# Feed-forward and routing of a graph layer: block 2's second layers ahead of block 3's first, routing steps moved up, ranks in another PSUM bank

## The chip, the core and the metric

One core of a Trainium2 chip runs the whole program. The metric is the device time of one execution in microseconds; the kernel before takes 1076.64 us (median of 3 runs, 1076.25 to 1078.03).

## What is computed

A graph layer over 2048 nodes of width 256 and a mixture of 8 experts behind it, both with a residual. The changed stage is the end of the first and the beginning of the second: the feed-forward of the graph layer, the layer norm behind it, and the routing of each node to its two best experts.

```python
    # graph layer: attention over adj, then
    ht = layer_norm(ht + attn, ln2_scale, ln2_bias)
    ff = gelu_tanh(ht @ W1) @ W2                 # W1 256x1024, W2 1024x256
    x = x + ht + ff
    # mixture of experts, on the normalised rows
    xn = _layernorm(x)
    gate_logits = xn @ gate_w.T                  # 8 experts
    topk_vals, topk_idx = top_k(gate_logits, 2)
    topk_w = softmax(topk_vals)
    for e in range(8):
        y = gelu(xn @ w1[e].T + b1[e]) @ w2[e].T + b2[e]
        out += comb[:, e:e + 1] * y              # comb: topk_w at topk_idx
    return x + out
```

## The kernel before

The program has two blocks of instruction streams, one stream for each engine, with semaphores between them written out by hand; at the end of a block every engine drains and all wait for each other. The first block does the attention (to about 660 us) and then the feed-forward and the routing; the second runs the experts over 23 slots of 256 or 128 rows.

The feed-forward works on four blocks b of 512 nodes (four tiles of 128, TPB). For block b:

- TensorE turns the normalised rows (turn_h2), makes the eight parts f of the hidden layer (hidden, six products each, in fp16 pairs) into PSUM banks 0 and 1, and the second layer for two halves r of the block (back, 48 products each, banks 4 and 5).
- ScalarE copies the turned rows (high_turned) and does the Gelu and the fp16 copy of each part f (hidden_high); VectorE makes the low half of each (split_turned, split_hidden). back(b, 0) needs all eight splits of its block. The split products of even and odd blocks lie in the places of expert weights 1 and 2 (gT[0], gT[1]), so SyncE loads expert set 1 behind back(2, 1) and set 2 behind back(3, 1).
- VectorE adds the second layer (ffn_sum), forms the new x (new_x), its moments (new_stats, new_moments); GpSimd makes the row factors from them (row_factors(1, b)); ScalarE normalises the four tiles (normalise_x) into rows, which has a buffer for even and one for odd blocks.
- TensorE turns the rows (turn_xn, banks 2 and 3), ScalarE copies them (copy_xnT), TensorE makes the gate logits (gates, bank 2).
- VectorE chooses the best and the second expert (choose_first, choose_second); TensorE counts the ranks of the nodes in each expert (ranks, bank 3); ScalarE makes the exponential of the gap between the two logits (gap_exponential); VectorE computes the weights and the target rows (send: slots).
- GpSimd scatters the rows to expert_rows, eight indirect DMAs for a block (scatter). normalise_x(b) for b of 2 or 3 waits until the scatter of block b - 2, which has the same buffer of rows, has landed.

The order in which each engine does these things is the order of the calls in its stream. Before, TensorE does turn_h2(3), the eight parts of hidden(3) with ranks(0) behind f = 4, back(2, 0), turn_xn(1), back(2, 1), gates(1), back(3, 0), ranks(1), back(3, 1), turn_xn(2), gates(2), ranks(2), turn_xn(3), gates(3), ranks(3). Since ranks(b) and the turned rows share bank 3, turn_xn(b) waits until VectorE has read the ranks of block b - 1 in send (rank_read; its last writer is place, L1159). ScalarE's exponentials need another activation table than the Gelus.

Of the kernel before, what the change touches and what calls it, by code (L numbers as in the profile page):

```python
# [6 lines left out]
ALU = mybir.AluOpType  # L7
# [24 lines left out]
def graph_attention_and_experts(nc, x, adj, adjT, nodemask, h_target, ln1_scale, ln1_bias, Wq, bq, Wk, bk, Wv, bv,  # L32
# [3 lines left out]
    DC = D // P  # L36
# [15 lines left out]
    with ctx:  # L52
# [335 lines left out]
        with block:  # L388
# [275 lines left out]
            def _(pool):  # L664
# [85 lines left out]
                def scatter(b):  # L750

                    pool.wait_ge(rows_ready, 2 * b + 2)
                    pool.wait_ge(slots_ready, 2 * b + 2)
                    for a in range(TPB):
                        for k in range(TOPK):
                            pool.indirect_dma_start(
                                out=expert_rows[:, :], in_=rows[:, b % 2, a, :], in_offset=None,
                                out_offset=bass.IndirectOffsetOnAxis(ap=slots[:, b % 2, k, a:a + 1], axis=0),
                                bounds_check=E * REGION - 1).then_inc(scattered[b % 2], 16)
# [95 lines left out]
                scatter(0)  # L855
                row_factors(1, 2)
                scatter(1)
                row_factors(1, 3)
                scatter(2)
# [5 lines left out]
            def _(dve):  # L865
# [274 lines left out]
                def send(b):  # L1140
# [16 lines left out]
                    then(dve.tensor_tensor(rank[:, :, :], ps[:, 3, 0:TPB * E].rearrange("p (a e) -> p a e", e=E),  # L1157
                                           place[:, :].unsqueeze(1).to_broadcast([P, TPB, E]), ALU.add))
                    dve.tensor_tensor(place[:, :], place[:, :], ps[:, 3, TPB * E:(TPB + 1) * E], ALU.add)\  # L1159
# [95 lines left out]
                ffn_sum(1, 0)  # L1255
                ffn_sum(1, 1)
                split_turned(3)
                for f in range(FC):
                    split_hidden(3, f)
                    if f in (0, 2):  # L1260
                        new_x(1, (f, f + 1))
                    elif f == 1:
                        choose_first(0)
                        dve.wait_ge(rank_read, 1)
                    elif f == 3:
                        choose_second(0)
                    elif f in (4, 5):
                        new_stats(1, (2 * f - 8, 2 * f - 7))
                    elif f == 6:
                        new_moments(1)  # L1270
                send(0)
                ffn_sum(2, 0)
                ffn_sum(2, 1)
                new_x(2, range(TPB))
                new_stats(2, range(TPB))
                new_moments(2)
                choose_first(1)
                choose_second(1)
                ffn_sum(3, 0)
                new_x(3, (0, 1))  # L1280
                send(1)
                ffn_sum(3, 1)
                new_x(3, (2, 3))
                new_stats(3, range(TPB))
                new_moments(3)
                choose_first(2)
                choose_second(2)
                send(2)
# [57 lines left out]
            def _(act):  # L1346
# [178 lines left out]
                for f in range(FC):  # L1525
                    hidden_high(3, f)
                gap_exponential(0)
                normalise_x(1)
                copy_xnT(1)
                gap_exponential(1)  # L1530
                normalise_x(2)
                copy_xnT(2)
                normalise_x(3)
                gap_exponential(2)
# [4 lines left out]
            def _(pe):  # L1539
# [144 lines left out]
                def turn_xn(b):  # L1684
                    pe.wait_ge(xn_ready, TPB * (b + 1))
                    if b:
                        pe.wait_ge(gates_read, b)
                        pe.wait_ge(rank_read, b + 1)
                    else:
                        pe.wait_ge(attn_added, 2 * NB)  # L1690
                    for c in range(DC):
                        for a in range(TPB):
                            mm = pe.transpose(ps[:, 2 + c, a * P:(a + 1) * P],
                                              rows[:, b % 2, a, c * P:(c + 1) * P], ident[:, :])
                    mm.then_inc(xnT_ready, 1)
# [9 lines left out]
                def ranks(b):  # L1705

                    pe.wait_ge(member_ready, b + 1)
                    for a in range(TPB):
                        for k in range(a + 1):
                            pe.matmul(ps[:, 3, a * E:(a + 1) * E], (before if k == a else onesb)[:, :],  # L1710
                                      member[:, k, :], start=(k == 0), stop=(k == a))
                    for k in range(TPB):
                        mm = pe.matmul(ps[:, 3, TPB * E:(TPB + 1) * E], onesb[:, :], member[:, k, :],
                                       start=(k == 0), stop=(k == TPB - 1))
                    mm.then_inc(rank_ready, 1)
# [84 lines left out]
                turn_h2(3)  # L1800
                for f in range(FC):
                    hidden(3, f)
                    if f == 4:
                        pe.wait_ge(c3_ready, 12)
                        ranks(0)
                back(2, 0)
                turn_xn(1)
                back(2, 1)
                gates(1)
                back(3, 0)  # L1810
                ranks(1)
                back(3, 1)
                turn_xn(2)
                gates(2)
                ranks(2)
                turn_xn(3)
# [253 lines left out]
```

## Time and profile before

| | |
|---|---|
| median of 3 runs | 1076.64 us |
| the profiled execution | 1077.44 us, of it 1075.7 us span |
| first block's stage after the attention | about 660 to 827 us of the span |
| TensorE (PE) busy | 947.6 us, 88% of the span |
| ScalarE (ACT) busy | 741.7 us, 69% |
| VectorE (DVE) busy | 660.1 us, 61% |
| GpSimd (POOL) busy | 542.6 us, 50% |

Times of rows are microseconds from the start of the span. A row of a timeline has start, duration, engine, line, operation, out<-in, shape, count, and in brackets the idle time of the engine before it and what released it. Matmuls overlap at their ends, so the next one can start before the end that a row shows. TensorE's granted clock is 1.00 at 2.4 GHz and 0.50 at 1.2 GHz.

### The profile page before, as it was taken

The numbers are of one execution on the slowest core, as the hardware profiler recorded it, in microseconds if no ns is written. First come the engines' busy times: TensorE is split into PE (matmuls) and PEld (weight loads), VectorE is DVE, ScalarE is ACT, GpSimd is POOL, SyncE is SP. The second block draws the span as 40 slices with busy tenths as digits, with TensorE's granted clock in tenths as the row PEclk, the third lists the DMA queues.
The fourth block names the chain that finished last, engine by engine and source line by source line (L and its number), as shares of the span: only waits on it lengthen the run. The fifth ranks groups of instructions, "written<-read, shape, count | busy, mean of one in ns | idle before, by whom it ended". The sixth has DMA issues, their size and how long they took to land. (4 is left out here: it accounts for less than half of the span.)

```text
span 1075.7 us, 20828 instructions
## 1 busy us (share of the span) xinstructions
PE 947.6 (88%) x6750; PEld 571.3 (53%) x6750; DVE 660.1 (61%) x1947; ACT 741.7 (69%) x949; POOL 542.6 (50%) x480
## 2 busy tenths in 40 slices
PE   2696999999999999999999978898930999999993
PEld 1353444444444444444444444464820898989872
DVE  7867677877778777787777635644643243434421
ACT  4644899999999999999999945653310645455551
POOL 6746576766767667676657872000453123232321
PEclk9998899999999999999999989998955999999997
DMA  9699436736366353673574554910642123232323
GB/s 283 185 288 278 152 125 229 237 132 195 124 236 227 134 195 120 229 239 114 189 263 172 170 187 136 420 66 20 210 165 78 38 46 62 42 59 40 47 37 94
DMA packets 74395, 168.43 MB, mean 157 GB/s; under 512 B 13619, under 2 KB 42419, under 8 KB 68403
## 3 DMA queue, kind: packets, MB, share of 16 engines
q1 hardware_dynamic: 50450, 97.99, 28.1%
q0 software_dynamic: 19984, 67.93, 21.0%
q10 hardware_dynamic: 3856, 1.19, 0.5%
q8 instruction: 58, 0.95, 0.4%
q14 instruction: 47, 0.38, 0.1%
HBM read 120.84 MB, written 61.96 MB: 170 GB/s over the span
## 5 line engine op out<-in xcount | busy, mean ns | idle before, releaser
L971 DVE CUSTOM_DVE_ANT_0 masked<-ps,maskA 128x512 f32<-128x512 f32 x512 | 347.5, 689 | 122.9 <-PE ps L1589 119.7
L1396 ACT ACTIVATE masked<-masked,negmax 128x2048 f32<-128x2048 f32 x128 | 256.4, 2003 | 24.6 <-DVE negmax L977 24.3
L1495 ACT ACTIVATE weights<-ps 128x1024 f32<-128x1024 f32 x256 | 253.5, 1014 | 25.3 <-PE ps L1614 22.6
L1589 PE MATMUL ps<-ks,qs 96*128 96x512 f32 x512 | 254.3, 533 | 9.4 <-DVE piecemax L971 8.0
L1612 PE MATMUL ps<-qs,ks 98*128 98x512 f32 x512 | 228.8, 506 | 8.7 <-DMA qs<-shift_lo 8.6
L1614 PE MATMUL ps<-maskB,identb 128*128 128x512 bf16 x512 | 201.5, 394 | 0.0
L1890 POOL DMA_INDIRECT sum_rows<-y,ids x39 | 60.3, 1547 | 174.7 <-DVE y L1928 157.4
L1589 PEld LDWEIGHTS ps<-ks,qs 96*128 96x128 f32 x512 | 98.7, 193 | 91.5 <-DVE piecemax L971 72.6
L1626 PE MATMUL ps<-weights,v_all 128*32 128x256 f32 x2048 | 137.1, 385 | 0.9 <-ACT weights L1495 0.9
L725 POOL TENSOR_SCALAR maskB<-adjB 128x1024 bf16<-128x1024 int32 x32 | 116.6, 3642 | 36.7 <-DMA adjB<-in_adjT 32.0
L1910 DVE TENSOR_TENSOR gT<-ffn_w,gT 128x2048 f16<-128x2048 f32 (+1 forms) x23 | 45.2, 1967 | 129.3 <-ACT gT L1967 129.3
L1614 PEld LDWEIGHTS ps<-maskB,identb 128*128 128x128 bf16 x512 | 50.0, 98 | 126.6 <-issue 122.3
L2002 PE MATMUL ps<-xT,wall 128*128 128x256 f16 (+1 forms) x1104 | 116.4, 260 | 0.2
L1612 PEld LDWEIGHTS ps<-qs,ks 98*128 98x128 f32 x512 | 100.7, 197 | 25.0 <-issue 12.8
L2014 PE MATMUL ps<-wall,gT 128*128 x936 | 106.3, 273 | 1.4 <-DVE y L1928 1.4
L2002 PEld LDWEIGHTS ps<-xT,wall 128*128 x1104 | 98.5, 98 | 15.6 <-issue 1.7
L1964 ACT ACTIVATE ffn_w<-ps,b1s 128x256 f32<-128x256 f32 (+1 forms) x184 | 70.7, 438 | 48.4 <-PE ps L2002 45.3
L731 POOL TENSOR_TENSOR total<-total,rT 64x256 f32<-64x256 f32 x32 | 23.5, 734 | 147.8 <-DVE total L959 147.8
L2014 PEld LDWEIGHTS ps<-wall,gT 128*128 128x128 f16 x936 | 90.7, 98 | 13.7 <-issue 1.9
L1626 PEld LDWEIGHTS ps<-weights,v_all 128*32 128x32 f32 x2048 | 53.4, 109 | 64.5 <-issue 40.7
L706 POOL TENSOR_TENSOR whl<-wch,whl 128x1024 f16<-128x1024 f32 x32 | 68.7, 2146 | 2.7
L1953 ACT ACTIVATE xT<-ps 128x512 f16<-128x512 f32 (+1 forms) x23 | 12.2, 531 | 76.8 <-PE ps L1989 76.8
(209 smaller groups left out, 1153.7 us busy)
## 6 DMA issues: line engine op xcount, KB each, us to landing
expert_rows<-pad_rows POOLq DMA_DIRECT2D x73, 272.0 KB, 5.8
split_weights<-whl POOLq DMA_DIRECT2D x36, 512.0 KB, 3.3
adjA<-in_adj SPq DMA_DIRECT2D x16, 1024.0 KB, 6.2
adjB<-in_adjT SPq DMA_DIRECT2D x32, 512.0 KB, 5.6
wall<-split_weights SPq DMA_DIRECT2D x16, 1024.0 KB, 15.1
wch<-in_w1T POOLq DMA_DIRECT2D x14, 512.0 KB, 6.3
wch<-in_w2T POOLq DMA_DIRECT2D x14, 512.0 KB, 6.0
xr<-expert_rows SPq DMA_DIRECT2D x16, 272.0 KB, 2.8
```

Of the source, the lines that this page charges most:

```text
L706: pool.tensor_tensor(whl[:, 1, :], chunk[:, :], whl[:, 0, :], ALU.subtract).then_inc(wch_split, 1)
L725: pool.tensor_scalar(maskB[:, b % 2, 2 * h:2 * h + 2, :], adjB[:, h % 2, :, :], 0.0, NO_EDGE, ALU.is_equal, ALU.mult).then_inc(maskB_next, 1)
L971: dve.tensor_tensor_reduce(masked[:, a % 2, k * 512:(k + 1) * 512], ps[:, u % 2, :], maskA[:, a, k * 512:(k + 1) * 512], 1.0, NO_EDGE, ALU ...
L1396: act.activation(masked[:, a % 2, :], masked[:, a % 2, :], ACT.Exp, bias=negmax[:, h % 2, a:a + 1], accum_out=rowsum[:, h % 4, a:a + 1]).t ...
L1495: act.activation(weights[:, j % 4, :, :], ps[:, 2 + 2 * (j % 2):4 + 2 * (j % 2), :], ACT.Exp).then_inc(weights_ready, 1)
L1589: pe.matmul(ps[:, u % 2, :], qs[0:KR, h % 4, a * P:(a + 1) * P], ks[0:KR, h, k * 512:(k + 1) * 512], start=True, stop=True)\
L1612: pe.matmul(bank, ks[:, h, (2 * j + i) * P:(2 * j + i + 1) * P], qs[:, h % 4, :], start=True, stop=False)
L1614: mm = pe.matmul(bank, identb[:, :], maskB[:, b % 2, 2 * j + i, :], start=False, stop=True)
L1626: mm = pe.matmul(ps[at:at + HD, 6 + h % 2, 0:TB // 2], v_all[:, 2 * j + i, h * HD:(h + 1) * HD], weights[:, j % 4, i, t * (TB // 2):(t + 1 ...
L1964: act.activation(g4[:, m, 0:w], ps[:, m // 2, m % 2 * PR:m % 2 * PR + w], ACT.Gelu, bias=b1s[:, e, m:m + 1], scale=1.0 / WSCALE).then_inc( ...
L2002: mm = pe.matmul(ps[:, m // 2, m % 2 * PR:m % 2 * PR + w], wall[:, e, 0, p, c * HE + m * P:c * HE + (m + 1) * P], xT[:, j % 2, x_, c, 0:w] ...
L2014: mm = pe.matmul(ps[:, 4 + a, 0:D], gT4[:, g, j % 2, m, a * P:(a + 1) * P], wall[:, e, 1, p, m * D:(m + 1) * D], start=(m == 0 and n == 0) ...
```

## The change

TensorE's order becomes turn_h2(3), back(2, 0), back(2, 1), ranks(0), turn_xn(1), the eight parts of hidden(3) with gates(1) behind f = 2, ranks(1), turn_xn(2), gates(2), back(3, 0), ranks(2), back(3, 1), turn_xn(3), gates(3), ranks(3). The ranks go to bank 6, which turn_h2 used; turn_xn no longer waits for rank_read, ranks does, and ranks(0) also waits for block 3's turned rows to be read. On VectorE the steps of block 1 and the choice of block 0 stand before the splits of block 3, ffn_sum(2) and send(0) too; the steps of block 2 and the choice of block 1 go between the splits. On ScalarE gap_exponential(0), normalise_x(1) and copy_xnT(1) stand before the Gelus of block 3, normalise_x(2) behind the Gelu of f = 5, gap_exponential(1) behind the last, and gap_exponential(2) before normalise_x(3). On GpSimd row_factors(1, 2) stands before the last tile of scatter(0) (its last two DMAs), and scatter(2) before row_factors(1, 3). No instruction of the computation is added or taken away. SyncE's stream is unchanged.

```diff
--- before.py
+++ after.py
@@ -747,11 +747,11 @@
                     pool.wait_ge(root3[k], b + 1)
                     pool.tensor_tensor(m[:, 8, :], m[:, 7, :], m[:, 3, :], ALU.mult).then_inc(rstd3[k], 1)
 
-                def scatter(b):
+                def scatter(b, tiles=range(TPB)):
 
                     pool.wait_ge(rows_ready, 2 * b + 2)
                     pool.wait_ge(slots_ready, 2 * b + 2)
-                    for a in range(TPB):
+                    for a in tiles:
                         for k in range(TOPK):
                             pool.indirect_dma_start(
                                 out=expert_rows[:, :], in_=rows[:, b % 2, a, :], in_offset=None,
@@ -852,11 +852,12 @@
                           allow_small_or_imprecise_dtypes=True).then_inc(c3_ready, 1)
                 pool.memset(base[:, 2 * E:2 * E + 1], float(E * REGION)).then_inc(c3_ready, 1)
                 pool.wait_ge(prefilled, 16 * (E * REGION // PR + 1))
-                scatter(0)
+                scatter(0, range(3))
                 row_factors(1, 2)
+                scatter(0, (3,))
                 scatter(1)
+                scatter(2)
                 row_factors(1, 3)
-                scatter(2)
                 scatter(3)
                 for q in range(2):
                     pool.wait_ge(scattered[q], 16 * TOPK * NT // 2)
@@ -1154,9 +1155,9 @@
                     dve.tensor_copy(rows[:, b % 2, :, D + E], tokens[:, b * TPB:(b + 1) * TPB])\
                         .then_inc(rows_ready, 1)
                     dve.wait_ge(rank_ready, b + 1)
-                    then(dve.tensor_tensor(rank[:, :, :], ps[:, 3, 0:TPB * E].rearrange("p (a e) -> p a e", e=E),
+                    then(dve.tensor_tensor(rank[:, :, :], ps[:, 6, 0:TPB * E].rearrange("p (a e) -> p a e", e=E),
                                            place[:, :].unsqueeze(1).to_broadcast([P, TPB, E]), ALU.add))
-                    dve.tensor_tensor(place[:, :], place[:, :], ps[:, 3, TPB * E:(TPB + 1) * E], ALU.add)\
+                    dve.tensor_tensor(place[:, :], place[:, :], ps[:, 6, TPB * E:(TPB + 1) * E], ALU.add)\
                         .then_inc(rank_read, 1)
                     for k in range(TOPK):
                         mark(dve.tensor_tensor(picked[:, k, :, :], hots[:, k, :, :], rank[:, :, :], ALU.mult))
@@ -1252,40 +1253,39 @@
                         new_stats(0, (2 * f - 4, 2 * f - 3))
                     elif f == 4:
                         new_moments(0)
-                ffn_sum(1, 0)
-                ffn_sum(1, 1)
+                for r in range(2):
+                    ffn_sum(1, r)
+                new_x(1, range(TPB))
+                new_stats(1, range(TPB))
+                new_moments(1)
                 split_turned(3)
+                choose_first(0)
+                dve.wait_ge(rank_read, 1)
+                choose_second(0)
+                for r in range(2):
+                    ffn_sum(2, r)
+                send(0)
                 for f in range(FC):
                     split_hidden(3, f)
-                    if f in (0, 2):
-                        new_x(1, (f, f + 1))
-                    elif f == 1:
-                        choose_first(0)
-                        dve.wait_ge(rank_read, 1)
-                    elif f == 3:
-                        choose_second(0)
-                    elif f in (4, 5):
-                        new_stats(1, (2 * f - 8, 2 * f - 7))
+                    if f < 2:
+                        new_x(2, (2 * f, 2 * f + 1))
+                    elif f < 4:
+                        new_stats(2, (2 * f - 4, 2 * f - 3))
+                    elif f == 4:
+                        new_moments(2)
+                    elif f == 5:
+                        choose_first(1)
                     elif f == 6:
-                        new_moments(1)
-                send(0)
-                ffn_sum(2, 0)
-                ffn_sum(2, 1)
-                new_x(2, range(TPB))
-                new_stats(2, range(TPB))
-                new_moments(2)
-                choose_first(1)
-                choose_second(1)
+                        choose_second(1)
+                send(1)
+                choose_first(2)
+                choose_second(2)
                 ffn_sum(3, 0)
-                new_x(3, (0, 1))
-                send(1)
+                send(2)
                 ffn_sum(3, 1)
-                new_x(3, (2, 3))
+                new_x(3, range(TPB))
                 new_stats(3, range(TPB))
                 new_moments(3)
-                choose_first(2)
-                choose_second(2)
-                send(2)
                 choose_first(3)
                 choose_second(3)
                 send(3)
@@ -1522,16 +1522,17 @@
                 normalise_x(0)
                 copy_xnT(0)
                 high_turned(3)
-                for f in range(FC):
-                    hidden_high(3, f)
                 gap_exponential(0)
                 normalise_x(1)
                 copy_xnT(1)
+                for f in range(FC):
+                    hidden_high(3, f)
+                    if f == 5:
+                        normalise_x(2)
                 gap_exponential(1)
-                normalise_x(2)
                 copy_xnT(2)
+                gap_exponential(2)
                 normalise_x(3)
-                gap_exponential(2)
                 copy_xnT(3)
                 gap_exponential(3)
 
@@ -1685,7 +1686,6 @@
                     pe.wait_ge(xn_ready, TPB * (b + 1))
                     if b:
                         pe.wait_ge(gates_read, b)
-                        pe.wait_ge(rank_read, b + 1)
                     else:
                         pe.wait_ge(attn_added, 2 * NB)
                     for c in range(DC):
@@ -1705,12 +1705,15 @@
                 def ranks(b):
 
                     pe.wait_ge(member_ready, b + 1)
+                    pe.wait_ge(rank_read, b + 1)
+                    if b == 0:
+                        pe.wait_ge(h2T_split, DC * NB)
                     for a in range(TPB):
                         for k in range(a + 1):
-                            pe.matmul(ps[:, 3, a * E:(a + 1) * E], (before if k == a else onesb)[:, :],
+                            pe.matmul(ps[:, 6, a * E:(a + 1) * E], (before if k == a else onesb)[:, :],
                                       member[:, k, :], start=(k == 0), stop=(k == a))
                     for k in range(TPB):
-                        mm = pe.matmul(ps[:, 3, TPB * E:(TPB + 1) * E], onesb[:, :], member[:, k, :],
+                        mm = pe.matmul(ps[:, 6, TPB * E:(TPB + 1) * E], onesb[:, :], member[:, k, :],
                                        start=(k == 0), stop=(k == TPB - 1))
                     mm.then_inc(rank_ready, 1)
 
@@ -1798,21 +1801,21 @@
                 pe.wait_ge(gw_in, 16)
                 gates(0)
                 turn_h2(3)
+                back(2, 0)
+                back(2, 1)
+                pe.wait_ge(c3_ready, 12)
+                ranks(0)
+                turn_xn(1)
                 for f in range(FC):
                     hidden(3, f)
-                    if f == 4:
-                        pe.wait_ge(c3_ready, 12)
-                        ranks(0)
-                back(2, 0)
-                turn_xn(1)
-                back(2, 1)
-                gates(1)
-                back(3, 0)
+                    if f == 2:
+                        gates(1)
                 ranks(1)
-                back(3, 1)
                 turn_xn(2)
                 gates(2)
+                back(3, 0)
                 ranks(2)
+                back(3, 1)
                 turn_xn(3)
                 gates(3)
                 ranks(3)
```

## Rows read from the trace of the kernel before

**Rows 1.** chain that ended last, in order of time: start, us, what

```profile
834.17 6.82 PE ps L2002 x48
```

**Rows 2.** GpSimd's queue at the boundary of the blocks (line 388)

```profile
L388 POOLq DRAIN  x1: 6608/6608/6608, 820.2 to 820.2; - x1
```

**Rows 3.** GpSimd's timeline: scatters (L756) and row factors of layer norm (L746, L748)

```profile
754.64 1.41 POOL L746 TENSOR_TENSOR mo<-mo,minus_half 128x4 f32<-128x4 f32 x1 [34.76 <-DVE mo L1047]
...
759.28 1.15 POOL L756 DMA_INDIRECT expert_rows<-rows,slots  x1 [2.75 <-issue]
...
768.43 0.97 POOL L756 DMA_INDIRECT expert_rows<-rows,slots  x1 [0.30 <-issue]
...
787.23 1.05 POOL L746 TENSOR_TENSOR mo<-mo,minus_half 128x4 f32<-128x4 f32 x1
788.35 0.20 POOL L748 TENSOR_TENSOR mo<-mo 128x4 f32<-128x4 f32 x1
...
808.50 0.97 POOL L756 DMA_INDIRECT expert_rows<-rows,slots  x1 [1.81 <-DVE slots L1166]
...
817.45 0.98 POOL L756 DMA_INDIRECT expert_rows<-rows,slots  x1 [0.30 <-issue]
```

**Rows 4.** VectorE's timeline: sum, moments, choice, send of several blocks

```profile
764.86 0.69 DVE L1088 SCALAR_TENSOR_TENSOR hb<-ps,hb 128x512 f32<-128x512 f32 x1 [5.61 <-PE ps L1679]
...
768.49 0.17 DVE L1040 TENSOR_TENSOR mo<-st 128x4 f32<-128x4 f32 x1
...
769.51 0.19 DVE L1124 COPY logits<-ps 128x32 f32<-128x32 f32 x1
...
771.08 0.19 DVE L1111 TENSOR_REDUCE top<-logits 128x4 f32<-128x32 f32 x1
...
772.20 0.19 DVE L1135 TENSOR_TENSOR member<-hot 128x32 bf16<-128x32 f32 x1
...
805.30 0.17 DVE L1143 TENSOR_SCALAR gap<-gap 128x4 f32<-128x4 f32 x1 [0.27 <-ACT gap L1443]
...
807.40 0.24 DVE L1166 CAST slots<-slotf 128x4 uint32<-128x4 f32 x2
```

**Rows 5.** TensorE's timeline: hidden(2), back(1,1), gates(0), turn_h2(3), turn_xn(3), gates(3)

```profile
708.40 10.54 PE L1668 MATMUL ps<-hT,ffn_w 128*128 128x512 f16 x48 [1.57 <-DVE hT L1075]
...
724.88 5.40 PE L1679 MATMUL ps<-ffn_w,wall 128*128 128x256 f16 x48
730.12 1.85 PE L1701 MATMUL ps<-gw,xnT 128*128 128x8 f32 x16
731.83 1.07 PE L1657 MATMUL ps<-ident,hb 128*128 128x128 f32 x8
...
795.24 1.94 PE L1693 MATMUL ps<-ident,rows 128*128 128x128 f32 x8 [9.24 <-DVE place L1159]
798.29 3.58 PE L1701 MATMUL ps<-gw,xnT 128*128 128x8 f32 x16 [1.11 <-ACT xnT L1439]
```

**Rows 6.** ScalarE's timeline: Gelu and copy, exponential, normalise_x(3)

```profile
709.97 0.60 ACT L1430 ACTIVATE g32a<-ps 128x512 f32<-128x512 f32 x1 [2.46 <-PE ps L1668]
710.59 0.63 ACT L1433 ACTIVATE wall<-g32a 128x512 f16<-128x512 f32 x1
...
754.48 1.28 ACT L1443 ACT_TABLE_LOAD   x1
755.78 0.21 ACT L1443 ACTIVATE gap<-gap 128x4 f32<-128x4 f32 x1
...
791.39 2.07 ACT L1410 ACTIVATE rows<-xb,mo 128x256 f32<-128x256 f32 x4 [11.25 <-DMA expert_rows<-rows,slots]
```

**Rows 7.** the scatters' line: from issue to landing

```profile
DMA to landing us min/median/max: 2.4/3.0/7.7
```

**Rows 8.** two stretches: length, each engine's busy time, granted clock, DMA share, GB/s

```profile
759.00:776.00 17.00, 16.32 (x162) 14.65 (x161) 10.49 (x47) 1.51 (x3) 9.23 (x10) 1.00 0.90 313
790.00:795.00 5.00, 0.00 (x0) 0.00 (x0) 1.24 (x9) 2.17 (x5) 0.00 (x0) 0.50 0.01 4
```

## Prediction

> **What bounds the kernel now.** I read the chain that ended last first. It goes back through the second block (the expert slots, TensorE nearly without a gap) and stops just ahead of that block's first products at 834.17 [rows 1], with the load of its first rows behind the boundary of the two blocks. So the question is what ends the first block. GpSimd's sequencer does: its drain, 6.61 us from 820.2, is the last thing there [rows 2]. GpSimd's timeline [rows 3] shows what it drains behind: scatter(3), eight indirect DMAs from 808.50 to 818.43. They follow send(3) on VectorE (slots written at 807.64 [rows 4]); send(3) follows gates(3) and turn_xn(3) on TensorE, which starts at 795.24 after a wait of 9.24 us for VectorE's place, that is for send(2) [rows 5]; send(2) waited for gap_exponential(2), which stands on ScalarE behind normalise_x(3), and this began at 791.39 after 11.25 us of waiting for scatter(1) to land [rows 6]. From turn_xn(3)'s start to the slots of send(3) are 12.40 us, and behind that nothing is changed: scatter(3), the drain and the second block follow as now. **The one number to find is the new start of turn_xn(3).** Each us later than 795.24 is a us on the span, 1075.7 in an execution of 1077.44; the median of the runs is 1076.64, so I add the shift to the median.
>
> **TensorE, first part.** Nothing differs up to turn_h2(3) at 731.83 [rows 5], which takes 0.87. back(2,0) and back(2,1) now follow at once, since block 2's products are split by 721 and ffn_sum(1,1) needs only back(1,1): a back costs 5.24, from 724.88 to the gates at 730.12 [rows 5]. So back(2,1) ends at 743.3 instead of 764.8, 21 us earlier, at the cost that hidden(3) starts at 744.4, 10 us later, behind ranks(0) (0.4) and turn_xn(1) (0.9). VectorE has the time for what is put before it: new_x, new_stats and new_moments of block 1, 3.6 with a sum (764.86 to 768.49 in [rows 4]) and 1.0 more, from 730.9 on, then split_turned(3) 1.2, choose_first 1.57 and choose_second 1.30: done at 739.1. GpSimd's row_factors(1,1) now sits at 735 before an idle queue and costs nothing; normalise_x(1) ends at 742.8 behind gap_exponential(0), before TensorE wants it at 743.6.
>
> **send(0)** follows ffn_sum(2,1) and takes 2.34 (805.30 to 807.64 in [rows 4]): slots of block 0 at 746.3 instead of 758.3. This is the gain of the change.
>
> **ScalarE.** gap_exponential(0) now stands before block 3's Gelus and gap_exponential(1) behind, so there are two table loads more, 1.28 each, with the next activation 0.02 behind [rows 6]. The one before the first Gelu (746.0 to 747.3) costs TensorE 0.8; the last is costed below. Pace after that: 1.30 per part of the hidden layer on TensorE (48 products in 10.54 for eight parts, [rows 5]), 0.60 + 0.63 on ScalarE [rows 6], 1.71 for gates(1) behind the third. So ScalarE is through f = 4 at 755.1 and f = 5 at 756.4. A stall of 0.8 and a stretch of gates could cost the clock here; as a bound 1.7 us.
>
> The Trainium skill (ScalarE: Activation LUTs, What ACT_TABLE_LOAD costs) adds a drain of 1.38 us to each switch of table sets, 2.66 in all; the trace shows 1.30 from the load to the next activation's start, so the measurement decides. By the page copy_xnT(2) would be some 0.5 us later, and the sum by as much.
>
> **The new wait.** normalise_x(2) now stands between f = 5 and f = 6 and waits for all eight scatters of block 0. Their queue is GpSimd: scatter(0) starts 0.9 after the slots, at 747.2; eight starts take 9.15 from first to last [rows 3], so six end at 754.8. Then row_factors(1,2) waits for new_moments(2), which VectorE writes behind f = 4's split, at 756.8; 1.41 as after idling, 0.3 for the second instruction and the handovers, make 758.5 (1.05 in place of 1.41 where GpSimd was not idle; both in [rows 3]). Only then come the last two scatters, at 758.8 and 760.1. A scatter lands 2.4 at best, 3.0 in the median and 7.7 at worst after its issue [rows 7]; I take 2.7, because the loads that are also pulled forward (x 0.5 MB, b2b 1 MB, expert set 1 2 MB, from 743 on, x1 0.5 MB, six scatters 0.8 MB) make 4.8 MB, and at the 313 GB/s of rows 8 they are through near 759, as the last scatters begin. So ScalarE stands idle from 756.4 to **762.8**, and what is queued behind it is hidden_high f = 6 and 7, and behind those, on VectorE, split f = 6 and choose_second(1), and on TensorE ranks(1), turn_xn(2), gates(2) and both back(3), none of which needs block 0's scatter. TensorE runs dry at 757.6. SyncE's stream keeps its order and only starts earlier; nobody waits for its loads before the second block.
>
> **From there.** normalise_x(2) 2.07 [rows 6]: 764.9. Gelu and copy of f = 6: 766.1; split 0.6, choose_second(1) to member 1.12 + 0.19 (771.08 to 772.20 in [rows 4]): 768.1. ranks(1) 0.4: 768.6. turn_xn(2) and the copy: at 795.24, after an idle TensorE, the turn took 1.94 at a granted clock of 0.50 (1.2 GHz), and the gates began 3.05 behind its start and took 3.58 [rows 5, 8]; full-clock gates took 1.85 [rows 5]. Here TensorE has been idle 10.5 us, so: gates 771.7, end 775.1. The exponential of block 1 (table load 768.1 to 769.4) is beside the turn and free at this clock. back(3,0) begins at 775.1 cold. In the second block the first 48 products of this shape after such a pause took 6.82 instead of 5.24 [rows 1, 5], with 3 us of cold work before them; back(3,0) has only gates before it, so I take 2.5 above 5.24 (bounds 1.6, and 5.2 if it stayed at half): 782.8.
> ffn_sum(3,0) 0.8, send(2) 2.34: 785.9. scatter(2) 0.9 later at 786.8; scatter(1) is through by then (slots(1) about 772.0, so 772.9 to 783). Eight scatters take 9.93 (808.50 to 818.43 in [rows 3]): 796.7. row_factors(1,3) now stands behind scatter(2), not before it: 1.3 [rows 3], 798.0. Its own input would be there at 793.9 (back(3,1) 788.5, then 4.7 as above plus the latency), so GpSimd's queue costs 3 us here. normalise_x(3) 2.1: 800.1, turn_xn(3) at **800.2**. The waits added to ranks cost nothing: block 3's turned rows are read by 736.3, long before ranks(0) at 743.2, and place of the block before is written before each ranks is due (send(0) 746, send(1) 772, send(2) 786, against ranks(1) to (3) at 768, 783 and 806). The bank change does its part: the turn no longer waits for send(2), which was 1.8 behind normalise_x(3) before.
>
> **Sum:** 800.2 − 795.24 = +4.9 us. 12 us are won at send(0); 6.4 go to ScalarE's wait, 2.5 each to cold gates and back(3,0), the rest to block 3's second layers standing behind block 2's gates and to GpSimd's queue. Predicted 1076.64 + 4.9 = **1081.5**.
>
> **Rivals.**
> *Late landing, slower still.* The last two scatters meet loads on the DMA engines. Before, with wall loads running, landings took up to 7.7 and the engines were 0.90 busy [rows 7, 8]. Then normalise_x(2) starts at 767.3, and everything shifts by 4.6: 1086.1. For it: the pulled-forward loads end only just before. Against: 759 is an upper estimate for most of the bytes, issued from 743 on. 0.15. The Trainium skill (DMA: Bandwidth & Descriptors, Queues, rings and completion order) says that each DMA engine takes turns between queues by packets, so a scatter shares with loads in flight; the landings from 2.4 to 7.7 agree.
> *Warm TensorE, about the same.* If the clock is full from ranks(1) on, back(3,0) starts at 772.5 and ends at 777.8; scatter(2) is then bound by scatter(1), 783.3 to 793.2, turn_xn(3) at 796.8: +1.5, 1078.1. Against: idle 10.5 us, where 9.2 us of idling left 0.50 [rows 5, 8]. Also a landing 3 us earlier gives this time. 0.14.
> *Faster.* ScalarE doesn't stand: the last scatter of block 0 lands by 756.4. Then the whole chain behind moves up 6.4: −1.5; and if TensorE, no longer dry, keeps its clock too, 3.4 more: −4.9, 1071.7. The sign turns at a landing of 757.9; below 756.4 an earlier landing wins nothing more, so a time 0.2% under needs the clock as well. Against: eight scatters from 747.2 and a landing of 2.4 [rows 3, 7] can't be done before 759. Only if send(0) came some 4 us sooner would it be; it hangs on back(2,1). 0.07, for a misread wait as well.
> *The forecast*, with landing 2.4 to 4.5 and back(3,0) 1.6 to 3.4 over its warm time: +3.5 to +7.5. 0.64.
>
> **Chances.** What a measurement of this kernel can tell from no change is about 0.2%, 2.15 us. Slower by more: the forecast and the late landing, 0.79; within: 0.14; faster: 0.07. The range takes in the warm case's edge and the late landing: 1077.8 to 1086.8.
>
> **What would show it.** In the profile after: send(0)'s slots near 746; a wait of normalise_x(2) for scatter(0) of about 6 us with TensorE dry beside it; two more table loads; gates(2) at half clock; row_factors(1,3) right behind scatter(2); turn_xn(3) near 800, with no wait for place. The forecast is wrong if normalise_x(2) doesn't wait, if TensorE is busy from 758 to 768, or if turn_xn(3) starts before 795.

## The result, and the profile after

The changed kernel takes 1082.85 us (median; 1076.41 for the kernel before beside it), a ratio of 1.0055 with the interval 1.0029 to 1.0081: 5.9 us slower, where 4.9 were forecast. The profiled execution has a span of 1082.2 us in 1084.0. Every ratio here is formed from fast runs against runs of the kernel before beside them; one of the twelve runs of e12, 2473.74 us, is slow for an unknown reason and left out.

What follows reads one stretch, from the start of turn_h2(3), behind which the streams differ, to the start of turn_xn(3), on which the end of the first block hangs. It is 63.41 us before [rows 5] and 68.49 after (734.36 to 802.85). So the stretch is 5.1 us longer. The spans differ by 6.5, because turn_h2(3) begins 2.5 us later in this execution, by the same instructions, and what follows turn_xn(3) takes 1.1 less. That the end hangs on turn_xn(3) holds throughout: in all fourteen profiles the first DMA of scatter(3) starts 13.0 to 13.5 us behind it, and the span ends 266.1 to 268.0 us behind that DMA.

GpSimd's timeline of the kernel after, to be held against [rows 3]:

```profile
749.81 1.15 POOL L756 DMA_INDIRECT expert_rows<-rows,slots  x1 [10.79 <-issue]
...
757.20 0.97 POOL L756 DMA_INDIRECT expert_rows<-rows,slots  x1 [0.30 <-issue]
759.31 1.42 POOL L746 TENSOR_TENSOR mo<-mo,minus_half 128x4 f32<-128x4 f32 x1 [1.14 <-DVE mo L1048]
760.81 0.20 POOL L748 TENSOR_TENSOR mo<-mo 128x4 f32<-128x4 f32 x1
761.62 1.05 POOL L756 DMA_INDIRECT expert_rows<-rows,slots  x1 [0.60 <-issue]
762.97 0.97 POOL L756 DMA_INDIRECT expert_rows<-rows,slots  x1 [0.30 <-issue]
774.46 0.97 POOL L756 DMA_INDIRECT expert_rows<-rows,slots  x1 [10.52 <-DVE slots L1167]
...
789.36 0.97 POOL L756 DMA_INDIRECT expert_rows<-rows,slots  x1 [4.99 <-DVE slots L1167]
...
798.31 0.98 POOL L756 DMA_INDIRECT expert_rows<-rows,slots  x1 [0.30 <-issue]
799.31 1.04 POOL L746 TENSOR_TENSOR mo<-mo,minus_half 128x4 f32<-128x4 f32 x1
```

scatter(0) begins 15.5 us behind turn_h2(3) instead of 27.5, the 12 us that the change was to win (7.6 against a second profile of the kernel before, e8, where it begins at 23.1); then GpSimd stands 10.5 and 5.0 us for slots, and row_factors(1,3) starts the moment scatter(2) is through. ScalarE's timeline says why the slots come late [rows 6]:

```profile
736.13 1.28 ACT L1443 ACT_TABLE_LOAD   x1
741.55 0.20 ACT L1443 ACTIVATE gap<-gap 128x4 f32<-128x4 f32 x1 [4.13 <-DVE gap L1138]
...
758.27 0.63 ACT L1433 ACTIVATE wall<-g32b 128x512 f16<-128x512 f32 x1
765.45 2.07 ACT L1410 ACTIVATE rows<-xb,mo 128x256 f32<-128x256 f32 x4 [6.55 <-DMA expert_rows<-rows,slots]
767.43 0.57 ACT L1430 ACTIVATE g32a<-ps 128x512 f32<-128x512 f32 x1
...
769.83 1.28 ACT L1443 ACT_TABLE_LOAD   x1
...
800.72 2.08 ACT L1410 ACTIVATE rows<-xb,mo 128x256 f32<-128x256 f32 x4 [19.56 <-POOL mo L748]
```

normalise_x(2) waits 6.55 us for the scatter, between the copy of f = 5 and the Gelu of f = 6. TensorE's timeline, beside it [rows 5], and a window over the ranks, the turn and the gates (length, busy time of PE, its weight loads, DVE, ACT and POOL, granted clock, DMA share, GB/s):

```profile
753.50 6.63 PE L1669 MATMUL ps<-hT,ffn_w 128*128 128x512 f16 x30
770.73 0.19 PE L1713 MATMUL ps<-member,before 128*128 128x8 bf16 x1 [10.60 <-DVE member L1136]
...
771.13 1.95 PE L1693 MATMUL ps<-ident,rows 128*128 128x128 f32 x8
774.19 3.58 PE L1701 MATMUL ps<-gw,xnT 128*128 128x8 f32 x16 [1.11 <-ACT xnT L1439]
777.62 8.00 PE L1680 MATMUL ps<-ffn_w,wall 128*128 128x256 f16 x48
...
802.85 1.97 PE L1693 MATMUL ps<-ident,rows 128*128 128x128 f32 x8 [11.64 <-ACT rows L1410]
```

```profile
770.70:778.00 7.30, 6.16 (x40) 5.63 (x41) 2.67 (x17) 1.64 (x3) 2.92 (x3) 0.50 0.11 40
```

TensorE is dry for 10.6 us, comes back at half clock (0.50), and does back(3,0) in 8.00 where a warm back takes 5.40. GpSimd's queue at the boundary of the blocks is unchanged, its drain has the same 6608 ns as in [rows 2]:

```profile
L388 POOLq DRAIN  x1: 6608/6608/6608, 827.6 to 827.6; - x1
```

### The profile page after: what moved, and what is told of

It is laid out like the page before. It is cut to its first block and busy times, and to the rows that moved or that the text cites. A ratio compares the mean times of both kernels' runs of the same rounds, so it can differ in the third digit from the quotient of the medians.

```text
span 1082.2 us, 20836 instructions
## 1 busy us (share of the span) xinstructions
PE 949.1 (88%) x6750; PEld 574.4 (53%) x6750; DVE 658.8 (61%) x1947; ACT 743.5 (69%) x951; POOL 542.9 (50%) x480
## 3 DMA queue, kind: packets, MB, share of 16 engines
q0 software_dynamic: 19984, 67.93, 21.1%
## 5 line engine op out<-in xcount | busy, mean ns | idle before, releaser
L2017 PEld LDWEIGHTS ps<-wall,gT 128*128 128x128 f16 x936 | 90.7, 98 | 13.5 <-issue 1.7
```

Of the source, the lines that this page charges most:

```text
L2017: mm = pe.matmul(ps[:, 4 + a, 0:D], gT4[:, g, j % 2, m, a * P:(a + 1) * P], wall[:, e, 1, p, m * D:(m + 1) * D], start=(m == 0 and n == 0) ...
```

## Experiments

The theory is the sum of the prediction: three waits in a row on one chain (normalise_x(2) for scatter(0); back(3) for that; row_factors(1,3) for scatter(2)), with a cold TensorE between. The rivals are that one of them is covered, or that the bank is what costs. Stretch and start of scatter(3) are counted from turn_h2(3) in each kernel's profiled execution; ratios are to the kernel before. e8 and e11 are one profiled run each, without a ratio.

| kernel | stretch | scatter(3) starts | ratio, interval |
|---|---|---|---|
| before | 63.41 | 76.67 | 1 |
| before, second profile (e8) | 59.10 | 72.37 | |
| changed | 68.49 | 81.53 | 1.0055 (1.0029 to 1.0081) |
| changed, second profile (e11) | 67.82 | 80.85 | |
| e1, normalise_x(2) behind the Gelus | 65.19 | 78.23 | 1.0054 (1.0029 to 1.0079) |
| e2, scatter(0) whole | 64.53 | 77.58 | 1.0057 (1.0034 to 1.0080) |
| e12, e2 again | 64.51 | 77.54 | 1.0021 (0.9998 to 1.0045) |
| e3, row factors first | 65.12 | 78.21 | 1.0038 (1.0014 to 1.0062) |
| e5, TensorE kept busy | 65.41 | 78.45 | 1.0064 (1.0044 to 1.0085) |
| e4, before with the bank alone | 57.31 | 70.79 | 0.9991 (0.9973 to 1.0009) |
| e6, e1 + e2 + e3 | 58.46 | 71.56 | 0.9978 (0.9964 to 0.9991) |
| e7, e6 and back(3) first | 50.37 | 63.85 | 0.9890 (0.9869 to 0.9911) |
| e9, e7 and the load later | 47.20 | 60.67 | 0.9849 (0.9828 to 0.9869) |
| e10, before with the load later | 56.49 | 69.76 | 0.9976 (0.9960 to 0.9991) |

**e1: normalise_x(2) behind the last Gelu.**

```diff
                 for f in range(FC):
                     hidden_high(3, f)
-                    if f == 5:
-                        normalise_x(2)
                 gap_exponential(1)
+                normalise_x(2)
                 copy_xnT(2)
```

> The changed kernel with normalise_x(2) behind the last Gelu part of block 3 and behind gap_exponential(1). Theory (ScalarE's wait for scatter(0) holds up the parts f = 6 and 7, and with them choose_second(1), ranks(1) and all behind): parts 6 and 7 follow f = 5 at once, ranks(1) stands near 763 instead of 770.7, and the chain then goes through normalise_x(2) itself, which still waits for the landing at about 765.4; so of the 6.5 us of waiting only some 3.5 come back: gates(2) begins near 770.7 instead of 774.2. From turn_h2(3) to turn_xn(3) 65.0 us instead of 68.5 (63.4 before), the time 3.5 us under the changed kernel's, 1.5 over the kernel before. Rival (the wait is covered by something else, GpSimd's queue): no difference, 68.5.

ScalarE's timeline of e1:

```profile
766.04 2.07 ACT L1410 ACTIVATE rows<-xb,mo 128x256 f32<-128x256 f32 x4 [3.54 <-DMA expert_rows<-rows,slots]
```

ranks(1) went from 36.4 us behind turn_h2(3) to 29 and normalise_x(2) still waited 3.54 us for the landing; the stretch is 3.3 us shorter, as expected (65.19 against 65.0). Nothing of it shows in the timed runs (1.0054). Taking ScalarE's stall away gives back half of its length, since the chain goes on through normalise_x(2) itself.

**e2 and e12: scatter(0) whole.**

```diff
-                scatter(0, range(3))
+                scatter(0)
                 row_factors(1, 2)
-                scatter(0, (3,))
                 scatter(1)
```

> The changed kernel with all four tiles of scatter(0) ahead of row_factors(1,2), as in the kernel before. Theory (normalise_x(2) waits for the last two scatters, which stand behind the wait for new_moments(2)): the last scatter is issued near 759.8 instead of 763.0, lands near 762.3 (the loads end near 758), row_factors(1,2) is done at about the same time, normalise_x(2) starts 3 us earlier, and the time is 3 us under the changed kernel's; turn_h2(3) to turn_xn(3) 65.5. Rival (the loads that were pulled forward slow the landing, so the earlier issue wins nothing): normalise_x(2) as now, 68.5, with landings of 5 us or more for the last two.

> e2 once more, unchanged: its profiled execution had the stretch from turn_h2(3) to turn_xn(3) 4.0 us shorter than the changed kernel's first and 3.3 shorter than its second, its timed runs lay as high as the changed kernel's (1.0057 to 1.0055). Theory (the stretch counts, and six runs with some 2 us of scatter each can't tell 3 us): stretch 64.5 to 66.2, time 1.0025 of the kernel before. Rival (without the profiler the stretch is another, and the order of the scatter wins nothing): 1.0055 again.

GpSimd's timeline of e2: the last scatter of block 0 goes out at 759.25, and row_factors(1,2) finds its input ready.

```profile
759.25 0.97 POOL L756 DMA_INDIRECT expert_rows<-rows,slots  x1 [0.30 <-issue]
760.25 1.06 POOL L746 TENSOR_TENSOR mo<-mo,minus_half 128x4 f32<-128x4 f32 x1
```

normalise_x(2) started at 761.73, 27.9 us behind turn_h2(3) instead of 31.1; the landing took 2.5. So the split of the scatter costs 3.2 us there, and the rival of a slow landing falls. The profiles agreed twice (64.53 and 64.51). The first set of timed runs gave 1.0057, the second 1.0021 (0.9998 to 1.0045); the intervals overlap, so the gain in time isn't settled by them.

**e3: row_factors(1,3) ahead of scatter(2).**

```diff
                 scatter(1)
-                scatter(2)
                 row_factors(1, 3)
+                scatter(2)
                 scatter(3)
```

> The changed kernel with row_factors(1,3) ahead of scatter(2), as in the kernel before. Theory (normalise_x(3) waits for row factors that stand behind eight scatters, 3 to 4 us after their input): row_factors(1,3) starts as soon as new_moments(3) is written, near 796.1 instead of 799.3; turn_xn(3) 3.2 us earlier; scatter(2) starts near 797.4 instead of 789.4 and ends near 807.3, before slots(3) at 811.8, so it costs nothing: turn_h2(3) to turn_xn(3) 65.3, the time 3.2 us under the changed kernel's. Rival (scatter(2) so late pushes scatter(3)): no gain, as scatter(3) would begin where it does now.

GpSimd's timeline of e3, where row_factors(1,3) waits for VectorE alone:

```profile
794.62 1.04 POOL L746 TENSOR_TENSOR mo<-mo,minus_half 128x4 f32<-128x4 f32 x1 [11.58 <-DVE mo L1048]
```

65.12 against 65.3, and GpSimd waited 4.7 us between scatter(2) and scatter(3): the queue cost 3.4 us, as read.

**e5: TensorE kept busy in the pause.** 44 more products ahead of ranks(1), into bank 7, which nobody reads.

```diff
+                for i in range(44):
+                    pe.matmul(ps[:, 7, :], hT[:, 1, 0, 0, 0:P], hT[:, 1, 0, 1, :], start=True, stop=True)
                 ranks(1)
                 turn_xn(2)
```

> The changed kernel with 44 products of 128x512 into an unread bank ahead of ranks(1), so that TensorE works through most of the time in which it stood dry (9.5 of 10.6 us). They change nothing in the output. Theory (gates(2) and back(3,0) are slow because the granted clock fell to 0.50 in that pause): turn_xn(2) about 1.05 instead of 1.95, gates(2) 1.85 instead of 3.58, back(3,0) 5.4 instead of 8.0, so back(3,0) ends 5 us earlier; scatter(2) is then bound by the end of scatter(1) at about 784.5 and starts 4.7 earlier: turn_h2(3) to turn_xn(3) 63.8, the time 4.7 us under the changed kernel's, about that of the kernel before. Rival (the cold clock is not on the path, GpSimd's queue is): 68.5 as now.

Windows of e5: the filler, turn and gates, and the two halves of back(3,0).

```profile
760.00:770.60 10.60, 9.50 (x46) 4.17 (x45) 2.81 (x14) 5.26 (x9) 2.77 (x4) 1.00 0.07 27
770.90:774.90 4.00, 2.89 (x31) 2.65 (x28) 2.26 (x15) 1.25 (x3) 0.63 (x1) 1.00 0.00 0
774.90:778.50 3.60, 3.60 (x23) 2.74 (x23) 2.54 (x14) 0.20 (x1) 2.69 (x4) 0.61 0.25 96
778.50:782.00 3.50, 3.50 (x37) 3.01 (x36) 0.00 (x0) 0.00 (x0) 2.59 (x4) 0.91 0.30 105
```

The turn took 1.07 and the gates 1.95, as a warm TensorE does them; but the clock fell behind them, and back(3,0) took 7.07 instead of 5.4. So 3.1 us of the stretch came back where 4.7 were expected, and nothing in the timed runs (1.0064). The pause makes turn and gates slow. That back(3,0) is half cold without the pause too, behind the turn, the wait of 1.1 us for copy_xnT and the gates, is seen in this one execution; in e4 and e10 the clock fell within the same gates behind the same wait (0.69 over 776.0 to 779.0, 0.64 over 778.3 to 781.3), while in both profiles of the kernel before it held through them. What makes it fall there isn't shown.

**e4: the bank alone, in the kernel before.** (ps[:, 3, ...] of the ranks becomes ps[:, 6, ...], four places, and:)

```diff
                     if b:
                         pe.wait_ge(gates_read, b)
-                        pe.wait_ge(rank_read, b + 1)
...
                     pe.wait_ge(member_ready, b + 1)
+                    pe.wait_ge(rank_read, b + 1)
+                    if b == 0:
+                        pe.wait_ge(h2T_split, DC * NB)
```

> The kernel before with one part of the change alone: ranks in bank 6, turn_xn without the wait for rank_read, ranks with it. Theory (turn_xn(3) waited 1.8 us for send(2) behind normalise_x(3), and nothing else hangs on the bank): turn_xn(3) starts right behind normalise_x(3), turn_h2(3) to turn_xn(3) 61.6 instead of 63.4; scatter(3) then starts 1.5 earlier, bound by the end of scatter(2); the time is 1.5 us under the kernel before. Rival (the second bank or the new waits cost something elsewhere, so the bank is the loss): slower than before.

turn_xn(3) now waits for normalise_x(3) alone, where [rows 5] has place:

```profile
789.26 1.97 PE L1692 MATMUL ps<-ident,rows 128*128 128x128 f32 x8 [7.05 <-ACT rows L1410]
```

61.6 were expected, counted from the first profile of the kernel before; 57.31 is 1.8 under the second (e8), in which the clock held in hidden(3) as here. So the bank is 1.8 us of the stretch and not the loss; as time it is too small for these runs (0.9973 to 1.0009).

**e8 and e11: both kernels once more**, unchanged.

> The kernel before once more, unchanged, for a second profile of it: how much the stretch from turn_h2(3) to turn_xn(3) (63.4 in the first) and the time of turn_h2(3) (731.8) differ between two executions of one kernel. In the first, the granted clock was 0.50 twice within hidden(3). Theory (the clock's falls hang on where the pauses lie, so they come again nearly alike): 62 to 65. Rival (they come by chance): a stretch shorter by up to 4 us, if both are missing.

> The changed kernel once more, unchanged, for a second profile. Theory (its two pauses of TensorE of over 10 us make it cold in the same places in each execution; only the phase in which the clock comes back differs): turn_h2(3) to turn_xn(3) within 1.7 us of 68.5. Rival (chance, as in the kernel before, whose two profiles differ by 4.3): a difference of 4 us.

The two windows over hidden(3), first in the first profile of the kernel before, then in the second:

```profile
734.50:743.00 8.50, 8.31 (x30) 3.21 (x30) 3.92 (x12) 4.91 (x8) 0.00 (x0) 0.80 0.00 0
745.90:753.20 7.30, 7.27 (x35) 3.10 (x36) 2.81 (x7) 2.46 (x4) 0.00 (x0) 0.59 0.07 23
```

```profile
736.00:743.00 7.00, 6.65 (x30) 2.86 (x30) 3.88 (x12) 4.91 (x8) 0.00 (x0) 1.00 0.00 0
746.00:750.50 4.50, 4.50 (x36) 2.34 (x35) 2.50 (x7) 2.57 (x5) 0.00 (x0) 1.00 0.07 25
```

The rival of e8 held: the falls of the clock within hidden(3) come in one execution and not in the other, at 4.3 us. e4 and e10 have the same order there and kept 1.00 too: back(2,0) begins 16.7 us behind turn_h2(3) in e4, e8 and e10 and 21.1 in the first profile, so the first is the one exception among four. In the changed kernel hidden(3) follows 10 us of second layers and kept 1.00, and its two executions differ by 0.7 only, which is back(3,0) (8.00 and 7.36).

**e6: e1, e2 and e3 together.**

> The changed kernel with the three orders of e1, e2 and e3 together: normalise_x(2) behind the Gelus, scatter(0) whole, row_factors(1,3) ahead of scatter(2). Theory (three waits in a row on one chain, so what they give adds up, less what e1 and e2 share at normalise_x(2)): normalise_x(2) 2 us earlier than in e1, turn_h2(3) to turn_xn(3) 59.8 instead of 68.5, the time 3.6 us under the kernel before. Rival (something else ends just behind, so that each alone gave its part but the sum doesn't): 64 or more, no better than before.

58.46 against 59.8, and faster than the kernel before in the timed runs (0.9978). What the three orders cost adds up: 10.0 us of the stretch, of 10.6 that they give singly, and 0.0077 of the time (8.3 us). That the earlier second layers win anything here isn't shown: e6 holds the new bank too, which alone measured 0.9991, and its scatter(3) starts 0.8 us earlier than in e8.

**e7: block 3's second layers ahead of block 2's gates**, on top of e6.

```diff
                 ranks(1)
+                back(3, 0)
                 turn_xn(2)
+                back(3, 1)
                 gates(2)
-                back(3, 0)
                 ranks(2)
-                back(3, 1)
                 turn_xn(3)
```

VectorE: choose_first(1) behind split_hidden(3, 2), choose_second(1) behind split_hidden(3, 5), and behind the splits:

```diff
                 send(1)
-                choose_first(2)
-                choose_second(2)
                 ffn_sum(3, 0)
-                send(2)
+                new_x(3, (0, 1))
+                new_stats(3, (0, 1))
                 ffn_sum(3, 1)
-                new_x(3, range(TPB))
-                new_stats(3, range(TPB))
+                new_x(3, (2, 3))
+                new_stats(3, (2, 3))
                 new_moments(3)
+                choose_first(2)
+                choose_second(2)
+                send(2)
                 choose_first(3)
```

ScalarE: normalise_x(3) ahead of gap_exponential(2).

> e6 and block 3's second layers ahead of block 2's gates: TensorE ranks(1), back(3,0), turn_xn(2), back(3,1), gates(2), ranks(2), turn_xn(3); VectorE chooses for block 1 from the third split of block 3 on and forms the moments of block 3 ahead of the choice of block 2; ScalarE normalise_x(3) ahead of gap_exponential(2). Theory (the rest of the change's loss is block 3's second layers standing behind normalise_x(2) and gates(2) on TensorE): back(3,0) starts 28 to 29 us behind turn_h2(3) instead of 43, turn_xn(3) 47 us instead of 68.5, scatter(3) follows scatter(2) at about 60.5 instead of 81.5 (76.7 before): the time 16 us under the kernel before, near 1060. Rival (GpSimd's scatters and the landing that normalise_x(3) waits for set the pace whatever TensorE does): turn_xn(3) no earlier than in e6.

TensorE's and then ScalarE's timeline of e7:

```profile
761.17 5.41 PE L1680 MATMUL ps<-ffn_w,wall 128*128 128x256 f16 x48 [0.77 <-DVE wall L1081]
766.42 1.04 PE L1693 MATMUL ps<-ident,rows 128*128 128x128 f32 x8
767.29 5.40 PE L1680 MATMUL ps<-ffn_w,wall 128*128 128x256 f16 x48
772.53 1.85 PE L1701 MATMUL ps<-gw,xnT 128*128 128x8 f32 x16
```

```profile
780.70 2.07 ACT L1411 ACTIVATE rows<-xb,mo 128x256 f32<-128x256 f32 x4 [12.18 <-DMA expert_rows<-rows,slots]
```

Both back(3) are warm, and the first begins 28.7 us behind turn_h2(3); the time is 1.1% under the kernel before. The orders of three engines change here at once, and what each is worth isn't known; nor is it whether they would win as much without the earlier back(2). The stretch is 50.4 instead of 47: the landing of scatter(1) came in between. Its last DMA, issued at 773.59, took 7.1 us, while expert set 2 was being loaded from 772.73 on; e9 tests whether that load is the reason.

**e9 and e10: that load later**, on e7 and on the kernel before.

```diff
+                store_x1(3)
                 sp.wait_ge(down_done, 2 * 4)
+                sp.wait_ge(xn_ready, TPB * NB)
                 load_expert_set(sp, 2)
-                store_x1(3)
```

> e7 with SyncE's load of expert set 2 (2 MB) behind the last normalise_x instead of behind back(3,1), and the store of the new x of block 3 ahead of it. Theory (in e7 normalise_x(3) waited 12.2 us for scatter(1), whose last DMA, issued at 773.6, landed only near 780.6 because that load began at 772.7): the landing takes 2.4 to 3.0, normalise_x(3) follows row_factors(1,3) 3.3 us earlier, scatter(3) 3.3 us earlier, turn_h2(3) to turn_xn(3) 47.1 instead of 50.4; the time 3.3 us under e7's. The load is still through by 795, 30 us ahead of the experts. Rival (the landing is slow for another reason, or the second block waits for the load): as e7, or slower.

> The kernel before with the same delay of the load of expert set 2. Theory: scatter(1)'s last landing takes 2.4 to 3.0 instead of 5.1, normalise_x(3) starts 2.5 us earlier and all behind it, turn_h2(3) to turn_xn(3) 56.6 to 60.9 as the clock falls (59.1 and 63.4 in the two profiles of the kernel before): the time 2.5 us under the kernel before. Rival: no difference, if the landing doesn't hang on that load.

ScalarE's timeline of e9:

```profile
778.43 2.07 ACT L1412 ACTIVATE rows<-xb,mo 128x256 f32<-128x256 f32 x4 [9.02 <-DMA expert_rows<-rows,slots]
```

The last landing took 3.9 in e9, more than the 2.4 to 3.0 expected, with the store of 0.5 MB beside it; it still came last, but only 0.1 us behind the row factors (778.31). The stretch is 47.2 (47.1 expected), at 1060.84 us the fastest kernel here, 1.5% under the kernel before. In the kernel before the same edit took the last landing from 5.1 to 2.5 us and gave 2.6 us of the stretch (against e8) and 0.9976 of the time, as expected.

## Why the prediction was right, point by point

Counted from turn_h2(3), with the prediction's time less 731.83 first and the trace of the kernel after behind it:

- *send(0)*: slots at 14.5; 14.4.
- *The new wait*: normalise_x(2) starts at 31.0; 31.1. The last scatter landed after 2.5 us (2.7 taken), the engines were free by then. e2 shows that the scatter's last two DMAs are what it waits for.
- *From there*: member at 36.3, gates(2) at 39.9, the end of back(3,0) at 51.0; 36.3, 39.8 and 51.1. The turn and the gates at half clock were right to 0.1. The 2.5 us for the cold back were 2.6, but 2.0 in the changed kernel's second profile: the hit within 0.1 is luck, the size isn't.
- *GpSimd's queue*: row_factors(1,3) at 64.9; 65.0, and 3.4 us of it came back in e3.
- *The sum*: the stretch 68.4; 68.49, and 67.82 in the second profile.

So the mechanism came as forecast, wait by wait. Three terms were off. **The base.** The shift was counted from one execution with a stretch of 63.41, in which the clock had fallen twice in hidden(3); the second one has 59.10. Of the 12 us that the sum puts down as won at send(0), 4.4 are those falls: against e8 scatter(0) starts 7.6 us earlier. Counted from e8 the predicted 68.4 would have been +9.3. By the mean of both profiles (61.25) and of the changed kernel's two (68.15) the change costs 6.9 us in the stretch, and by e8 alone 9.0; the timed 5.9 has an interval of 2.8 to either side, which holds the forecast and the 6.9 and leaves the 9.0 just outside. How often the clock falls there without the profiler isn't known, so that the sum came within 1 us of the timed difference is in part luck. That the first execution lay 0.8 over the median was no measure of what its stretch held. **The share of ScalarE's stall.** The prediction put 6.4 us on it; e1 gave 3.3, because normalise_x(2) is next on the chain anyway. **The table loads.** The prediction has block 1's behind the wait for its gap, at 36.3; it began at 35.5, straight behind the last copy, and block 0's ran at 736.13, 5 us ahead of its activation. The Gelus' load did begin behind its wait, at 14.2 as predicted. This changed no term.

Of the rivals, the late landing did not come for the two scatters that normalise_x(2) waits for, but it is real: e7 met it with 7.1 us, one stage later. The warm TensorE was sized at 3.4 us; e5 measured 3.1, without the whole back getting warm. The faster case did not come: it needed the last landing 24.6 us behind turn_h2(3), and it came at 31.1. e6, e7 and e9 are faster than the kernel before by other orders, not by that condition.

What stays open: e1, the first e2 and e5 lay as high as the changed kernel in their timed runs, though their profiles have 3.1 to 4.0 us less in the stretch. The runs of one kernel differ by 3 to 10 us among each other, a repeat of e2 came out at 1.0021, and e6 has the sum in both; whether single orders win less without the profiler isn't settled. The profiled executions differ by as much outside the stretch: e1's is 2.6 us shorter up to scatter(3) than the changed kernel's second, but begins turn_h2(3) 1.0 later and takes 1.4 more from scatter(3) on, so that the spans are 1079.4 and 1079.6.

## What to carry to other kernels

A step that waits for a buffer to be free should stand behind the work that doesn't need it: here one normalise between two Gelus held up ScalarE, and VectorE and TensorE behind it. Such a wait isn't worth its whole length, though: of 6.55 us 3.3 came back, because the chain goes on through the same step. When work is pulled forward, follow each queue that it joins, since what is late next is often a transfer or a helper's short instruction behind a row of DMAs. Take more than one profile of the kernel before as the base when the effect is under 1%: here the single one was the exception among four.

## What was not expected of the hardware

The clock came back and fell at different places in two executions of the same instructions, 4.3 us of one stretch. In e5 it fell to 0.61 over 3.6 us although TensorE had worked through the pause: what came last before were the turn, a wait of 1.1 us and the gates. An indirect DMA of 128 rows landed in 2.5 us with the DMA engines 0.07 busy over 760.0 to 771.1 (the changed kernel's last two of block 0), in 7.1 beside a load of 2 MB and a store of 0.5 MB (e7), and in 3.9 beside the store without the load (e9).
